# A two-layer decoder on one core: the order of work in the first expert layer and in the fused expert loop

## The chip, the core and the metric

One core of one Trainium2 chip. The metric is the device time in microseconds of one execution; the kernel has one launch. Everything is float32 where it matters here.

## The reference, cut to what matters

A decoder with two post-norm layers over 16 sequences of 64 tokens, 1024 tokens of width 256. Each layer is attention, cross-attention and an expert layer, each followed by a layer norm. The change touches the two expert layers.

```
# layer 0: 8 experts, the best 2 per token, hidden width 1024
probs = softmax(gelu(x @ rw1) @ rw2);  wgt, idx = top_k(probs, 2)
for e in range(8):
    Ye = gelu(x @ w1[e] + b1[e]) @ w2[e] + b2[e]
    Ce = gelu(b1[e]) @ w2[e] + b2[e]              # what a token gets that did not choose e
    for k in range(2):
        mask = idx[..., k] == e;  active = any(mask)
        out += active * wgt[..., k] * where(mask, Ye, Ce)

# layer 1: 64 gates mapped to 8 fused experts of 8 parts each, rank 8, hidden width 176
scores -> top 6 -> w_dense -> flat = w_dense[:, inv_mapping];  scalar = flat.sum(-1);  w = softmax(flat)
fused_linear(x, W, qa, qb, scale, w) = x @ W.T + scale * sum_k w_k * (x @ qa_k) @ qb_k
xe   = x + w @ muW.T
gate = silu(fused_linear(xe, gate...));  up = fused_linear(xe, up...)
y   += scalar * fused_linear(gate * up, down...)
# and a shared expert of width 352 on every token
```

## The kernel before, in words

The program is written engine by engine. TensorE (`pe`), VectorE (`dve`), ScalarE (`act`), GpSimd (`pool`) and SyncE (`sp`, which issues transfers) each run their own list in order, and semaphores (`Signal`) join them. There is no scheduler: the order on an engine is the order in the text. A float32 product is two instructions in the trace, each with a weight load of its own.

**First expert layer.** The router's logits give VectorE the marks of the chosen experts (L2252 to L2263). TensorE counts them (`c["before"]` and `c["ones"]`, L1199 and L1201), VectorE works out a place for each token and two tables, `in_lane` and `in_tile` (L2272 to L2295), and TensorE's product of the two (L1207) is the token list: 23 row tiles (`ROW_TILES`) of 128 tokens sorted by expert. GpSimd gathers each tile's rows (L720) and later scatters the answers (L728). SyncE fetches each tile's first weights (L589).

The constant term is what tokens get of experts they did not choose. `unseen(e)` (L1127) sums gelu(b1) @ w2 for expert e into four column quarters of bank 3; it needs all of `w2`, whose last two experts arrive late (L580). `sum_unseen` (L1136) adds the quarters, VectorE copies the 8 rows to `ceb` (L2331), under which `b2` lies. The weights of tokens (`weight_c`, 16 columns for each token tile) are transposed (L1219) to `wct`, copied by ScalarE (L1833). The counts for "is the expert active at all" are L1211, behind the token list.

Then comes the loop over row tiles (L1224). Tile r: `turn_rows(r+1)` transposes the next tile, `up(r)` makes 32 products into banks 0 and 1, `down(r-1)` 16 into bank 4 or 5. For r from 2 to 9 `turn_rows` also makes the constant term of one token tile (L1151), 16 rows deep, into the second half of its bank, and VectorE adds it to x (L2333).

**Fused expert loop.** 16 steps (`STEPS`), two halves of 512 tokens for each of 8 experts. Step n needs, on TensorE: the x products (`fuse_in`, L1569: w @ muW, 8 rows deep, one product for each half of the width), the rank products a (`ranks`, L1576), the gate and up features g and u and the tails t of both (`features`: L1588 from x, L1592 from the ranks; gate's ranks are rows 0 to 63 and up's 64 to 127), and the outputs (`outputs`: L1613 down's ranks d, over column halves, 128 rows of `h6` and 48 of `ha6`, L1618 and L1622 the sums over both). The list in step s is:

```
fuse_in(step + 1);  features(step);  ranks(step + 1);  outputs(step - 1)
```

All but the output sums go through four banks in turn (`ring`, L525): a product may start when the one four places earlier has been read (`bank_free`, L538). ScalarE reads g and t (silu, L2034), GpSimd scales them (L805), VectorE does the rest in this order: x of step s+1 is added to the tokens (`inputs6`, L2636; at the first half of an expert also L2643 and L2644, which scale its weights), u of s is multiplied with the gate (`hidden6`, L2653), a of s+1 with the weights (`ranks6`, L2661), t of s (L2653 again), d of s-1 (`down_ranks6`, L2669). The transfers of an expert and its mixing weights are issued by SyncE two steps or more ahead (L642, L661, L662). GpSimd clears `ha6` before the loop (L797).

## Time and profile before

| | us |
|---|---|
| median of three runs | 1045.49 |
| the three runs | 1042.62, 1056.3, 1045.49 |
| profiled execution, device time | 1040.52 |
| its span | 1038.6 |

| engine | busy us | share | instructions |
|---|---|---|---|
| TensorE | 958.0 | 92% | 7302 |
| TensorE weight loads | 594.0 | 57% | 7302 |
| VectorE | 541.3 | 52% | 1083 |
| ScalarE | 362.9 | 35% | 729 |
| GpSimd | 213.7 | 21% | 259 |

The span is from the first to the last instruction of the profiled execution; the device time holds some 2 us around it. A line number such as L1588 is the line of the kernel's text. "Busy" of TensorE is from an instruction's start to its modelled end, and neighbours overlap. The chain of waits is followed back from the last instruction: at each step it names what released the engine, or the instruction ahead of it. 68% of this chain is TensorE, 21% VectorE, 4% ScalarE. The mean granted clock of TensorE is 0.974 of its full 2.4 GHz; its lower level is 0.5.

### The profile page before, as it was taken

To read this page: it belongs to the slowest core of one execution; us is meant where nothing else is said; L and a number is where in the kernel's file an instruction comes from. 1 tells how busy PE (TensorE), PEld (TensorE's weight loads), DVE (VectorE), ACT (ScalarE), POOL (GpSimd) and SP (SyncE) were. 2 spreads that over 40 slices of the span, in tenths; PEclk is the share of its full clock that TensorE was granted. 3 is DMA by queue.
4 is the path that set the end of the run, shared out by engine and by line. 5 is a ranking of instruction groups with operands and counts; after the bars stand their busy time and mean duration, and the time that the engine had idled before them with its cause. 6 is when DMAs were issued, how large, how long until landed. Compare 5 with 4: busy or idle time off the path is not lost.

```text
span 1038.6 us, 18579 instructions
## 1 busy us (share of the span) xinstructions
PE 958.0 (92%) x7302; PEld 594.0 (57%) x7302; DVE 541.3 (52%) x1083; ACT 362.9 (35%) x729; POOL 213.7 (21%) x259
## 2 busy tenths in 40 slices
PE   7799899999989999999888899878899999999995
PEld 3665543333458899997554467746554444444453
DVE  2589788988441110113788677758663232332325
ACT  2334536666522223333477245245230000000002
POOL 6011100000012222312125842730000111111110
PEclk9999999999989999999999999999799999999998
DMA  5000330000345555645130201230105033332001
GB/s 210 1 3 1 119 136 2 2 2 2 122 149 211 164 185 177 185 148 171 48 42 1 81 2 42 83 145 3 51 13 128 0 93 93 92 93 88 6 0 42
DMA packets 28602, 81.43 MB, mean 78 GB/s; under 512 B 10068, under 2 KB 17372, under 8 KB 22500
## 3 DMA queue, kind: packets, MB, share of 16 engines
q1 hardware_dynamic: 26308, 74.20, 21.9%
q0 software_dynamic: 2208, 6.03, 1.9%
q8 instruction: 60, 0.98, 0.4%
q14 instruction: 26, 0.21, 0.1%
HBM read 70.62 MB, written 8.55 MB: 76 GB/s over the span
## 4 chain that ended last, share of the span: by engine, by line
PE 68%; DVE 21%; ACT 4%; issue 3%; POOL 2%; DMA 1%; DVEq 0%; SPq 0%; ACTq 0%; POOLq 0%
PE psum L1588 9%; PE psum L1164 8%; PE psum L1176 8%; DVE arena L2185 5%; PE psum L1592 3%; PE psum L878 3%; PE psum L1383 3%; PE psum L1618 3%; PE psum L1576 3%; PE psum L1622 3%; PE psum L1554 2%; PE psum L1062 2%; DVE arena L2102 2%; DVE arena L2101 2%; PE psum L1613 2%
## 5 line engine op out<-in xcount | busy, mean ns | idle before, releaser
L2034 ACT ACTIVATE arena<-psum 128x512 f32<-128x512 f32 (+1 forms) x32 | 19.0, 593 | 219.5 <-PE psum L1592 219.5
L1842 ACT ACTIVATE arena<-psum,arena 128x128 f32<-128x128 f32 x184 | 52.4, 368 | 115.4 <-PE psum L1164 78.5
L1588 PE MATMUL psum<-arena 128*128 128x512 f32 (+1 forms) x192 | 90.6, 608 | 0.5 <-DVE arena L2653 0.5
L805 POOL TENSOR_TENSOR arena<-arena 128x512 f32<-128x512 f32 (+1 forms) x32 | 40.4, 1264 | 234.5 <-ACT arena L2034 234.5
L2185 DVE TENSOR_REDUCE arena<-psum 128x2 f32<-128x512 f32 x128 | 82.5, 688 | 11.0 <-PE psum L1008 9.5
L1164 PE MATMUL psum<-arena 128*128 128x128 f32 x736 | 86.8, 276 | 0.5 <-DVE arena L2328 0.5
L1164 PEld LDWEIGHTS psum<-arena 128*128 128x128 f32 x736 | 84.0, 192 | 3.4 <-issue 2.7
L1176 PE MATMUL psum<-arena 128*128 x368 | 83.4, 378 | 0.0
L2328 DVE COPY arena<-psum 128x256 f32<-128x256 f32 x23 | 9.7, 424 | 136.5 <-PE psum L1149 86.0
L1819 ACT ACTIVATE arena<-psum 128x1024 f32<-128x1024 f32 x64 | 65.3, 1024 | 30.4 <-PE psum L1030 27.1
L1176 PEld LDWEIGHTS psum<-arena 128*128 128x128 f32 x368 | 67.9, 189 | 9.0
L2653 DVE TENSOR_TENSOR arena<-arena,psum 128x512 f32<-128x512 f32 (+1 forms) x32 | 22.1, 689 | 86.9 <-POOL arena L805 86.4
L1588 PEld LDWEIGHTS psum<-arena 128*128 128x128 f32 (+1 forms) x192 | 33.1, 185 | 55.2 <-issue 53.5
L816 PE MATMUL psum<-arena 128*128 128x512 f32 (+1 forms) x118 | 50.9, 554 | 0.0
L1008 PE MATMUL psum<-arena 32*128 32x256 f16 x256 | 44.5, 276 | 5.8 <-DVE arena L2185 2.7
L728 POOL DMA_INDIRECT returned<-arena x23 | 22.7, 987 | 123.5 <-DVE arena L2344 123.5
L2636 DVE TENSOR_TENSOR arena<-psum,arena 128x512 f32<-128x512 f32 x32 | 22.1, 692 | 49.7 <-issue 45.8
L737 POOL TENSOR_TENSOR arena<-arena 128x512 f32<-128x512 f32 x32 | 32.9, 1054 | 45.9 <-ACT arena L1900 27.4
L878 PE MATMUL psum<-arena 64*128 64x256 f32 x256 | 33.1, 399 | 6.5 <-DVE arena L2132 5.9
L1062 PE MATMUL psum<-arena 128*32 128x256 f32 x512 | 35.1, 393 | 0.6 <-ACT arena L1819 0.5
L1592 PE MATMUL psum<-arena 64*128 64x512 f32 (+1 forms) x96 | 34.4, 625 | 0.0
L816 PEld LDWEIGHTS psum<-arena 128*128 128x128 f32 (+1 forms) x118 | 19.3, 169 | 26.2 <-issue 25.8
(357 smaller groups left out, 1764.2 us busy)
## 6 DMA issues: line engine op xcount, KB each, us to landing
arena<-in_w SPq DMA_DIRECT2D x31, 1024.0 KB, 9.9
arena<-in_experts SPq DMA_DIRECT2D x8, 1248.0 KB, 6.0
arena<-mixed SPq DMA_DIRECT2D x16, 256.0 KB
arena<-mixed SPq DMA_DIRECT2D x8, 512.0 KB, 9.3
arena<-returned SPq DMA_DIRECT2D x8, 256.0 KB, 4.5
kept<-arena SPq DMA_DIRECT2D x2, 1024.0 KB, 7.8
arena<-kept SPq DMA_DIRECT2D x2, 1024.0 KB, 5.9
arena<-in_w_ffn SPq DMA_DIRECT2D x1, 1152.0 KB, 5.1
```

Of the source, the lines that this page charges most:

```text
L805: do(pool.tensor_tensor(out=g6[rows, 2 * half + i, :], in0=g6[rows, 2 * half + i, :], in1=scale6[rows, f % BUFS, cols], op=ALU.mult), scaled6)
L816: pe.matmul(bank(spare), eye, wide(eye, 1, BANK // P), start=True, stop=True)
L878: last = pe.matmul(replicated(u, p)[:, g * D:(g + 1) * D], w[rows, g, :], qr[rows, u % 2, i, :], start=(i == 0), stop=(i == 1), tile_posit ...
L1008: last = pe.matmul(bank(u % 2)[:, tc * D:(tc + 1) * D], stack["q"][r0:r1, b, g, tc * P:(tc + 1) * P], stack["k"][r0:r1, b, g, :], start=Tr ...
L1062: last = pe.matmul(bank(6)[32 * q:32 * q + 32, 0:D], vx[:, b, sc, q, 32 * g:32 * g + 32], ptx[:, (n + q // 2) % 4, q % 2, sc, :], start=(g ...
L1164: last = pe.matmul(bank(n)[:, i * P:(i + 1) * P], w1_tile[:, r % 2, k, features], xst[:, r % 2, k, :], start=(k == 0), stop=(k == KC - 1))
L1176: last = pe.matmul(bank(4 + r % 2)[:, 0:D], hidt[:, r % 2, ic * P:(ic + 1) * P], w2v[:, bass.ds(e, 1), ic, :], start=(ic == 0), stop=(ic = ...
L1588: pe.matmul(out, e[w][:, k, :], xe6[:, half, k, :], start=(k == 0), stop=False)
L1592: mid_ps.by(pe.matmul(out, qb6[r0:r1, n // 2 % 2, q0:q0 + m], aw6[r0:r1, half, :], start=False, stop=True))
L1819: ptx_ready.by(act.activation(ptx[:, n % 4, :, :, :].rearrange("p a b c -> p (a b c)"), bank(2 + 2 * (n % 2), 2), ACT.Exp, scale=float(DHX ...
L1842: last = act.activation(hidt[:, r % 2, ic * P:(ic + 1) * P], bank(n)[:, i * P:(i + 1) * P], ACT.Gelu, bias=b1_tile[:, r % 4, ic:ic + 1])
L2185: ax_max.by(dve.tensor_reduce(nmx[:, b % 2, :, h], bank(u % 2).rearrange("p (t s) -> p t s", t=2), AX.X, ALU.max, negate=True))
```

## The change

In the first expert layer: the counts L1211 and `unseen(6)` go ahead of the token list's product, `unseen(7)` and two products without a use follow it (`keep_clock`). The transposed weights, `ceb` and `b2` now exist four times, one in each row quarter, so that the constant terms of four token tiles are four products side by side (`const_rows`); there are two such groups, in tiles 2 and 4, and VectorE adds each in two instructions (`add_const`). In the fused loop: `fuse_in(step + 1)` moves into `features`, between the rank products of g and u and the tails. Its two operands move from rows 0 and 32 to row halves, with zeros up to 64 rows, for which GpSimd clears `wm6`, and the 48 rows of `dqat` and `ha6` become 128. The ring's order follows.

```diff
--- before.py
+++ after.py
@@ -66,7 +66,7 @@
 
 EXPERT = [("gw", P, (KC, P)), ("uw", P, (KC, P)), ("tw", P, (KC, TAILS)), ("qa", P, (KC, P)),
           ("qb", P, (P + TAILS,)), ("qs", P, (P + TAILS,)), ("dw", P, (D,)), ("dwx", P, (D,)),
-          ("dqa", P, (KX * RX,)), ("dqat", TAIL, (KX * RX,)), ("ds", P, (D,)), ("mu", 32 + KX, (P,))]
+          ("dqa", P, (KX * RX,)), ("dqat", P, (KX * RX,)), ("ds", P, (D,)), ("mu", P, (P,))]
 
 
 def columns(parts):
@@ -311,6 +311,7 @@
         ce4_sb = again("ce4_sb", ov0_sb, B)
         ce_sum = again("ce_sum", o0_ps, B)
         tiles_ready = again("tiles_ready", q_sb, 6)
+        const_ps = again("const_ps", elu_ready, 1)
         rows_out = signal("rows_out")
         xs_in = [signal("xs_in_even"), signal("xs_in_odd")]
         xst_ps = again("xst_ps", mem_ps, NT)
@@ -386,8 +387,8 @@
         ti1_blank = again("ti1_blank", lg_ps, 1)
         unit_act = again("unit_act", p_exp, 1)
         unit_pool = again("unit_pool", p_sub, 1)
-        rest_ps = again("rest_ps", wct_ps, 2)
-        rm1_ready = again("rm1_ready", wct_sb, 2)
+        rest_ps = again("rest_ps", wct_ps, 1)
+        rm1_ready = again("rm1_ready", wct_sb, 4)
         solve_ps = again("solve_ps", cnt_ps, 2)
         xv_act = again("xv_act", ce_ps, 1)
         xv_dve = again("xv_dve", ceb_sb, 1)
@@ -522,7 +523,7 @@
         STEPS = 2 * FX
         ring, by_dve, by_act = {}, {}, {}
         for step in range(-1, STEPS + 1):
-            for kind, n in (("x", step + 1), ("g", step), ("u", step), ("t", step), ("a", step + 1), ("d", step - 1)):
+            for kind, n in (("g", step), ("u", step), ("x", step + 1), ("t", step), ("a", step + 1), ("d", step - 1)):
                 for k in range(KC if kind == "x" else 1):
                     if 0 <= n < STEPS:
                         ring[(kind, k), n] = len(ring)
@@ -576,7 +577,8 @@
                 fetch_expert(e, w12_early)
             sp.wait_ge(x_norm.sem, 2 * NT)
             sp.dma_start(a["rows"].rearrange("(j p) d -> p j d", p=P), x).then_inc(rows_out.sem, 16)
-            sp.dma_start(ceb[E0:2 * E0, :], a["b2"]).then_inc(b2_in.sem, 16)
+            for q in range(4):
+                sp.dma_start(ceb[32 * q + E0:32 * q + 2 * E0, :], a["b2"]).then_inc(b2_in.sem, 16)
             for e in range(len(EARLY), E0):
                 fetch_expert(e, w12_in[e])
             b1_at = columns(PACKS["w_route0"][:2])
@@ -640,7 +642,7 @@
                 mixed, buf = a["mixed"], f % BUFS
                 few = mixed[f * KX:(f + 1) * KX, :]
                 for k in range(KC):
-                    sp.dma_start(wm6[32 * k:32 * k + KX, buf, :], few).then_inc(near_in[buf].sem, 16)
+                    sp.dma_start(wm6[64 * k:64 * k + KX, buf, :], few).then_inc(near_in[buf].sem, 16)
                 for half in range(2):
                     sp.dma_start(we6[64 * half:64 * half + 64, buf, :], wide(few, 1, RX)).then_inc(mix_in[buf].sem, 16)
                 sp.dma_start(scale6[:, buf, :], mixed[FX * KX + f:FX * KX + f + 1, :].to_broadcast([P, B * S]))\
@@ -654,6 +656,7 @@
                     sp.wait_ge(wt6_sb.sem, wt6_sb.base + 2)
                     sp.dma_start(a["mixed"], wt6[0:FX * KX + FX, :]).then_inc(mixed_out.sem, 16)
                     sp.wait_ge(mixed_out.sem, 16)
+                    sp.wait_ge(tail_blank.sem, 1)
                     for near in range(BUFS):
                         fetch_mix(near)
                     continue
@@ -794,6 +797,7 @@
                 pool.wait_ge(xt_ps.sem, 2 * NT + j + 1)
                 x_beta.by(pool.tensor_tensor(out=x[:, j, :], in0=x[:, j, :], in1=x1["beta"], op=ALU.add))
             pool.wait_ge(x_norm.sem, 5 * NT)
+            do(pool.memset(wm6.rearrange("p a n -> p (a n)"), 0.0))
             do(pool.memset(ha6.rearrange("p a n -> p (a n)"), 0.0), tail_blank)
             for n in range(STEPS):
                 f, half = n // 2, n % 2
@@ -1135,22 +1139,29 @@
 
             def sum_unseen():
                 pe.wait_ge(ce4_sb.sem, ce4_sb.base + 1)
-                ce_sum.by(pe.matmul(bank(2)[0:E0, 0:D], c["selmax"][:, 0:E0, 0], ce4, start=True, stop=True))
+                for q in range(4):
+                    last = pe.matmul(bank(2)[32 * q:32 * q + E0, 0:D], c["selmax"][:, 0:E0, 0], ce4, start=True, stop=True,
+                                     tile_position=(0, 32 * q))
+                ce_sum.by(last)
 
             def turn_rows(r):
                 pe.wait_ge(xs_in[r % 2].sem, xs_in[r % 2].base + 16 * (r // 2 + 1))
                 if r >= 2:
                     pe.wait_ge(xst_sb.sem, xst_sb.base + r - 1)
-                if r == 2:
-                    pe.wait_ge(ceb_sb.sem, 1)
-                if 4 <= r < NT + 4:
-                    pe.wait_ge(const_read.sem, r - 3)
+                if r in (4, 6):
+                    pe.wait_ge(const_read.sem, r - 2)
                 for k in range(KC):
                     last = pe.transpose(bank(6 + r % 2)[:, k * P:(k + 1) * P], xs[:, r % 2, k * P:(k + 1) * P], ident)
-                if 2 <= r <= NT + 1:
-                    last = pe.matmul(bank(6 + r % 2)[:, D:2 * D], wct[0:2 * E0, (r - 2) * P:(r - 1) * P], ceb[0:2 * E0, :],
-                                     start=True, stop=True)
                 xst_ps.by(last)
+
+            def const_rows(half):
+                pe.wait_ge(ceb_sb.sem, 1)
+                pe.wait_ge(xst_sb.sem, xst_sb.base + 2 * half + 4)
+                for q in range(4):
+                    rows, b, at = slice(32 * q, 32 * q + 2 * E0), (2, 3, 6, 7)[q], (0, 0, D, D)[q]
+                    last = pe.matmul(bank(b)[:, at:at + D], wct[rows, half * P:(half + 1) * P], ceb[rows, :], start=True,
+                                     stop=True, tile_position=(32 * q, 0))
+                const_ps.by(last)
 
             def up(r):
                 pe.wait_ge(w1_in[r % 2].sem, w1_in[r % 2].base + 32 * (r // 2 + 1))
@@ -1201,35 +1212,40 @@
             cnt_ps.by(pe.matmul(bank(6)[:, 0:E0 * (NT + 1)], c["ones"], earlier[:, :, 0:NT + 1], start=False, stop=True))
             for e in EARLY[3:]:
                 unseen(e)
+            for j in range(NT):
+                last = pe.matmul(bank(5)[:, 0:2 * E0], c["ones"], marks[:, j, :], start=(j == 0), stop=(j == NT - 1))
+            cnt_ps.by(last)
+            pe.wait_ge(w12_in[6].sem, w12_in[6].base + 16)
+            unseen(6)
             for half in range(2):
                 pe.wait_ge(lanes_ready.sem, half + 1)
                 for n in range(half * NT, (half + 1) * NT):
                     last = pe.matmul(bank(4)[:, 0:ROW_TILES], in_lane[:, n, :], in_tile[:, n, :], start=(n == 0),
                                      stop=(n == 2 * NT - 1))
             spots_ps.by(last)
-            for j in range(NT):
-                last = pe.matmul(bank(5)[:, 0:2 * E0], c["ones"], marks[:, j, :], start=(j == 0), stop=(j == NT - 1))
-            cnt_ps.by(last)
-            for e in range(len(EARLY), E0):
-                pe.wait_ge(w12_in[e].sem, w12_in[e].base + 16)
-                unseen(e)
+            pe.wait_ge(w12_in[7].sem, w12_in[7].base + 16)
+            unseen(7)
+            keep_clock(2, 7)
             pe.wait_ge(wc_ready.sem, 1)
             for i in range(2):
-                for t in range(4):
-                    last = pe.transpose(bank(i)[0:2 * E0, t * P:(t + 1) * P], weight_c[:, 4 * i + t, :], ident)
-                wct_ps.by(last)
+                for q in range(4):
+                    last = pe.matmul(bank(0)[32 * q:32 * q + 2 * E0, i * P:(i + 1) * P], weight_c[:, 4 * i + q, :], ident,
+                                     start=True, stop=True, tile_position=(0, 32 * q))
+            wct_ps.by(last)
             pe.wait_ge(tiles_ready.sem, tiles_ready.base + 1)
-            pe.wait_ge(b2_in.sem, b2_in.base + 16)
+            pe.wait_ge(b2_in.sem, b2_in.base + 64)
             turn_rows(0)
             for r in range(ROW_TILES + 1):
                 if r + 1 < ROW_TILES:
                     turn_rows(r + 1)
                 if r == 0:
-                    pe.wait_ge(wct_sb.sem, 2)
+                    pe.wait_ge(wct_sb.sem, 4)
                 if r < ROW_TILES:
                     up(r)
                 if r == 0:
                     sum_unseen()
+                if r in (2, 4):
+                    const_rows(r // 2 - 1)
                 if r >= 1:
                     down(r - 1)
             def project5(u):
@@ -1565,7 +1581,7 @@
                 for k in range(KC):
                     bank_free(pe, (("x", k), n))
                 for k in range(KC):
-                    rows = slice(32 * k, 32 * k + KX)
+                    rows = slice(64 * k, 64 * k + 64)
                     mid_ps.by(pe.matmul(bank(ring[("x", k), n] % 4), ex[f % BUFS]["mu"][rows, :], wm6[rows, f % BUFS, cols],
                                         start=True, stop=True))
 
@@ -1597,6 +1613,8 @@
                 pe.wait_ge(qb6_ready.sem, qb6_ready.base + 2 * (n // 2) + 2)
                 from_ranks(gate, 0, 64, 0, P)
                 from_ranks(up, 64, P, 0, P)
+                if n + 1 < STEPS:
+                    fuse_in(n + 1)
                 from_ranks(from_x("t", "tw", TAILS), 0, P, P, TAILS)
 
             def tile_sum(j):
@@ -1611,7 +1629,7 @@
                     for u in range(2):
                         cols = slice(u * D, (u + 1) * D)
                         last = pe.matmul(bank(ring[key] % 4)[64 * u:64 * u + 64, 0:D], e[("dqa", "dqat")[i]],
-                                         (h6[:, half, cols], ha6[0:TAIL, half, cols])[i],
+                                         (h6, ha6)[i][:, half, cols],
                                          start=(i == 0), stop=(i == 1))
                 mid_ps.by(last)
                 for t in range(4):
@@ -1673,9 +1691,7 @@
             shared_down(1, (2, 3))
             pe.wait_ge(tail_blank.sem, 1)
             for step in range(STEPS + 1):
-                if step + 1 < STEPS:
-                    fuse_in(step + 1)
-                if 0 <= step < STEPS:
+                if step < STEPS:
                     features(step)
                 if step + 1 < STEPS:
                     ranks(step + 1)
@@ -1828,10 +1844,10 @@
                 r1_sb.by(act.activation(r1[:, n * BANK:(n + 1) * BANK], bank(2 + n), ACT.Gelu))
             act.wait_ge(p_sub.sem, 1)
             p_exp.by(act.activation(prob, prob, ACT.Exp))
-            for i in range(2):
-                act.wait_ge(wct_ps.sem, i + 1)
-                wct_sb.by(act.activation(wct[0:2 * E0, i * BANK:(i + 1) * BANK], bank(i)[0:2 * E0, :],
-                                         ACT.Copy))
+            act.wait_ge(wct_ps.sem, 1)
+            for q in range(4):
+                rows = slice(32 * q, 32 * q + 2 * E0)
+                wct_sb.by(act.activation(wct[rows, 0:2 * P], bank(0)[rows, 0:2 * P], ACT.Copy))
             for r in range(ROW_TILES):
                 if r >= 2:
                     act.wait_ge(down_ps.sem, down_ps.base + r - 1)
@@ -2328,15 +2344,24 @@
                 xst_sb.by(dve.tensor_copy(xst[:, r % 2, :, :].rearrange("p k t -> p (k t)"), bank(6 + r % 2)[:, 0:D]))
                 if r == 1:
                     dve.wait_ge(ce_sum.sem, ce_sum.base + 1)
-                    do(dve.tensor_copy(ceb[0:E0, :], bank(2)[0:E0, 0:D]), ceb_sb)
-                if 2 <= r <= NT + 1:
-                    const_read.by(dve.tensor_tensor(out=x[:, r - 2, :], in0=bank(6 + r % 2)[:, D:2 * D],
-                                                    in1=x[:, r - 2, :], op=ALU.add))
+                    for q in range(4):
+                        last = dve.tensor_copy(ceb[32 * q:32 * q + E0, :], bank(2)[32 * q:32 * q + E0, 0:D])
+                    do(last, ceb_sb)
+
+            def add_const(half):
+                dve.wait_ge(const_ps.sem, const_ps.base + half + 1)
+                for i, at in enumerate((0, D)):
+                    tiles = slice(4 * half + 2 * i, 4 * half + 2 * i + 2)
+                    const_read.by(dve.tensor_tensor(
+                        out=x[:, tiles, :], in0=bank((2, 6)[i], 2).rearrange("p (t c) -> p t c", t=2)[:, :, at:at + D],
+                        in1=x[:, tiles, :], op=ALU.add))
 
             copy_rows(0)
             for r in range(ROW_TILES + 2):
                 if r + 1 < ROW_TILES:
                     copy_rows(r + 1)
+                if r in (2, 4):
+                    add_const(r // 2 - 1)
                 if r >= 2:
                     dve.wait_ge(down_ps.sem, down_ps.base + r - 1)
                     if r >= 4:
@@ -2839,8 +2864,10 @@
             "qa": chunks(np.concatenate([rank("L1_ffn_gate_qa", f), rank("L1_ffn_up_qa", f)], 1)),
             "qb": fused(unrank("L1_ffn_gate_qb", f), unrank("L1_ffn_up_qb", f)), "qs": fused(*scales),
             "dw": dw[:P], "dwx": np.concatenate([dw[P:], np.zeros((64 - TAIL, D), np.float32), unrank("L1_ffn_down_qb", f)]),
-            "dqa": dqa[:P], "dqat": dqa[P:], "ds": every(g["L1_ffn_down_scale"][f]),
-            "mu": np.concatenate([mu[:, :P], np.zeros((32 - KX, P), np.float32), mu[:, P:]])}))
+            "dqa": dqa[:P], "dqat": np.concatenate([dqa[P:], np.zeros((P - TAIL, KX * RX), np.float32)]),
+            "ds": every(g["L1_ffn_down_scale"][f]),
+            "mu": np.concatenate([part for half in (mu[:, :P], mu[:, P:])
+                                  for part in (half, np.zeros((64 - KX, P), np.float32))])}))
     w["experts"] = np.stack(experts)
     w["x"] = g["x"].reshape(B * S, D)
     w["x_t"] = chunks(w["x"].T)
```

## Rows read from the trace of the kernel before

**Rows 1.** Chain of waits, one pass of the fused loop: start us, us, engine, line, count.

```profile
860.30 1.06 PE psum L1569 x4
861.36 3.63 PE psum L1588 x8
864.99 1.06 PE psum L1592 x4
866.05 1.90 PE psum L1588 x4
867.95 0.86 PE psum L1592 x2
868.81 1.72 PE psum L1576 x4
870.53 1.16 PE psum L1613 x8
871.69 1.92 PE psum L1618 x8
```

**Rows 2.** Timeline, the same pass, other engines: start us, us, engine, line, operation, idle before.

```profile
861.45 1.42 DVE L2636 TENSOR_TENSOR arena<-psum,arena 128x512 f32<-128x512 f32 x2 [3.54 <-issue]
...
863.34 0.42 DVE L2644 TENSOR_TENSOR arena<-arena 64x256 f32<-64x256 f32 x1
...
866.08 0.60 ACT L2034 ACTIVATE arena<-psum 128x512 f32<-128x512 f32 x1 [11.68 <-PE psum L1592]
...
866.82 1.26 POOL L805 TENSOR_TENSOR arena<-arena 128x512 f32<-128x512 f32 x1 [11.01 <-ACT arena L2034]
...
868.22 0.19 PEld L1576 LDWEIGHTS psum<-arena 128*128 128x128 f32 x1 [0.25 <-issue]
```

**Rows 3.** Timeline, TensorE, the loop's first turn.

```profile
801.15 3.27 PE L1588 MATMUL psum<-arena 128*128 128x512 f32 x7 [0.52 <-DVE arena L2653]
```

**Rows 4.** Chain of waits at the same place.

```profile
801.15 3.70 PE psum L1588 x8
```

**Rows 5.** Chain of waits, first expert layer.

```profile
307.01 0.42 DVE arena L2331
...
324.14 0.62 PE psum L1151 x2
324.76 3.77 PE psum L1164 x32
...
379.88 3.57 PE psum L1164 x32
```

**Rows 6.** Windows: length, busy PE, PEld, DVE, ACT, POOL (count), clock, DMA share, GB/s.

```profile
288.60:291.10 2.50, 0.02 (x1) 0.03 (x2) 2.36 (x6) 0.00 (x0) 0.00 (x0) 1.00 0.20 33
292.60:296.30 3.70, 3.70 (x24) 3.70 (x24) 1.65 (x8) 0.00 (x0) 1.60 (x2) 0.50 0.96 338
```

**Rows 7.** Chain of waits, from the token list to the first row tile.

```profile
292.99 3.42 PE psum L1211 x16
296.41 3.53 PE psum L1130 x32
...
302.63 3.81 PE psum L1164 x32
```

**Rows 8.** Timeline, TensorE, row halves in the first layer's attention.

```profile
119.57 2.00 PE L878 MATMUL psum<-arena 64*128 64x256 f32 x16
```

**Rows 9.** Timeline, TensorE, row quarters.

```profile
537.79 1.17 PE L1311 MATMUL psum<-arena 32*128 32x128 f32 x32
```

**Rows 10.** Timeline, GpSimd, the second gather.

```profile
295.86 0.95 POOL L720 DMA_INDIRECT arena<-rows,arena  x1 [0.30 <-issue]
```

**Rows 11.** All gathers of L720: issue to landing.

```profile
DMA to landing us min/median/max: 2.7/2.8/3.8
```

**Rows 12.** Timeline, GpSimd and VectorE, side by side.

```profile
583.14 3.04 POOL L737 TENSOR_TENSOR arena<-arena 128x512 f32<-128x512 f32 x3
...
584.39 0.69 DVE L2430 TENSOR_TENSOR arena<-psum,arena 128x512 f32<-128x512 f32 x1
```


## The prediction

> **What bounds the kernel now.** I read the chain of waits first. In the fused expert loop it never leaves TensorE: one pass of the loop is nine groups of products with no other engine between them [rows 1]. A full product of 512 columns takes two instructions of 0.43 us (four in 1.72, L1576), one of 256 columns two of 0.215. Against that the groups split by rows or columns of the array are dear where they meet the others: the x products (L1569) do four instructions two at a time, 2 x 0.43 = 0.86, and take 1.06; the eight full ones behind them should take 3.43 and take 3.63; the rank products L1592 (1.06) and the four behind them (1.90 for 1.72) show the same. So each island of row-split products costs about 0.40 beyond its streaming, 0.20 going in and 0.20 coming out. The reader should see that a step holds three islands: x, the gate and up ranks, and the column-split L1613.
>
> Then the timeline of the other engines in the same step [rows 2]: VectorE adds the x products 0.09 after their end, ScalarE takes the gate 0.03 after the ranks' end at 866.05, GpSimd's scaling ends at 868.08. All is idle enough today. The first turn of the loop is the exception: TensorE waits 0.52 there for VectorE [rows 3].
>
> In the first expert layer the chain is TensorE's too [rows 5]: a row tile with its constant term pays 0.62 for L1151 and 3.77 where a later tile pays 3.57 for the same 32 products, 0.82 in all, eight times. Before its first tile the windows show 2.5 us in which TensorE is all but idle, and behind it a granted clock of 0.50, the 1.2 GHz level [rows 6], in which L1211 and L1130 take 3.42 and 3.53 [rows 7].
>
> **The loop, part by part.** *x products between the ranks and the tails.* Both now use row halves 0 to 63 and 64 to 127, so two islands become one: 0.40 saved in each of the 15 steps that have an x product, 6.0 us. This takes for granted that four row-split passes follow one another without exposing their weight loads. The nearest row is sixteen 64-row instructions of 256 columns in 2.00 us [rows 8]: 8 x 0.215 = 1.72, and the rest is the way in and the last one's end. Nothing is exposed between them. The Trainium skill (TensorE: Matmul & The Clock Gate, "The mechanism" in Part 3) says that a weight load overlaps running products only when its row group differs. By it each further pass pair on the same halves would expose a load; the trace disagrees, since there loads and products alternate on the same two halves.
>
> *Zero rows instead of 48- and 8-row operands.* Rows cost no time, columns do. L1613 takes 1.16 and what follows it 1.92 [rows 1], where streaming is 4 x 0.215 + 8 x 0.215 = 2.58: 0.50 of excess, 0.10 more than the 0.40 of an island. I put that 0.10 down to the turn from 128 to 48 rows inside it, gone now: 16 x 0.1 = 1.6 us (between 0 and 2.4). The expert's transfer keeps its size, since the packed array already held 128 rows. The clearing of wm6 on GpSimd lies before the loop, in a stretch where that engine idles, and costs nothing; if it did not, SyncE's new wait on it would hold up the first mixes.
>
> *The ring of four banks.* Its order becomes g, u, x, x, t, a, d. The first turn no longer stops: g(1) now needs only x(1) read, not the tail t(0). Today that wait comes behind an x group, and goes: 0.5. Two new waits appear. t(n) needs g(n) read by ScalarE: 0.63 after the ranks' end, while the x products keep TensorE for 0.86. Covered. And a(n+1) needs u(n) read by VectorE (L2653). I lay one step out on the clock of [rows 1, 2]. Ranks end 866.05, x products 866.91, tails (1.90 + 0.86) 869.67; a's first weights would load 0.59 ahead of its slot as now (868.22 [rows 2] for 868.81 [rows 1]), at 869.08. VectorE adds x from 867.00 to 868.42 and only then, by its own order, multiplies u: 868.45 to 869.14 (0.69, as a sum of this shape has in [rows 12]). That is 0.06 late for the load and still 0.3 before the slot at 869.67: no loss. But when the next step starts an expert, L2643 and L2644 stand between (862.87 to 863.76, 0.89): u is read at 870.03. Behind such a wait eight products took 3.70 instead of 3.43 [rows 4], 0.27 from the release. So a streams from 870.03 + 0.04 + 0.27 = 870.34, 0.67 late. Seven steps are so (n+1 = 2, 4, ... 14): 4.7 us lost. Bounds: 0 if TensorE's queue or a short step covers it, 7 x 0.9 = 6.3 if the whole 0.89 shows. Behind a, VectorE and TensorE are late together, and nothing more is lost.
>
> Loop: 6.0 + 1.6 + 0.5 - 4.7 = 3.4 us gained.
>
> **The first expert layer.** *Constant term in two groups.* Removed: 8 x 0.82 = 6.6. Added: twice four products of 256 columns on four row quarters at once. A row for four quarters in float32 is 32 instructions of 128 columns in 1.17 [rows 9]: 8 x 0.107 = 0.86 and the way in. So a group is 0.43 + 0.40 = 0.83, two of them 1.7. Saved 4.9; if the four did not overlap, 2 x (1.71 + 0.4) = 4.2 would leave 2.4. VectorE's four additions of 128x512 (0.69 each) replace eight; they put off the copy of ys(0) and ys(2) by a product group, some 6 us, and with it a scatter and a gather on GpSimd's queue, but the gather is wanted two tiles later, over 10 us off. down(2) needs ys(0) a whole tile later too.
>
> *The wait for ceb.* turn_rows(2) waited for L2331 (0.42, with a hand-over of some 0.06 on either side [rows 5]); now not: 0.55 saved, less 0.1 for the four-quarter sum. VectorE's three further copies (3 x 0.42) end within up(1).
>
> *Counts ahead of the token list.* L1211 fills the idle 2.5 us [rows 6]; at the full level it is half of 3.42, 1.7, and the 16 instructions of expert 6 are a quarter of what 3.53 bought, 0.9. So they end near 291.3, before the second half of the lanes, whose product ends where L1211 starts today, at 292.99 [rows 7], and the list is not late. In front of expert 6's weights stand three more small transfers on SyncE's queue; today they are long there when used. Behind the list there is expert 7 (0.9) and two clock products (1.7), then the eight small products, now on column quarters. By then the gathers decide: the second is issued at 295.86 [rows 10] and lands after 2.8 to 3.8 [rows 11], so it is there at 298.7 to 299.7. up(0), today at 302.63 [rows 7], starts near 299.6: 3.0 saved. From it I take 0.8 for the clock, which may still be granted low for a stretch, as the engine stays thinly used until 299: 2.2 (0.5 to 3.5).
>
> Layer: 4.9 + 0.45 + 2.2 = 7.5 us.
>
> **Sum.** 3.4 + 7.5 = 10.9 us. The profiled execution took 1040.5 (span 1038.6), so 1029.6; the median of the runs, 5 us above it, goes to 1045.5 - 10.9 = 1034.6.
>
> **The rivals.**
> A, the late u costs nothing (chance 0.16): for it speaks that 0.67 hangs on the order of three short operations. Then 4.7 more is gained: 1030.
> B, the clock stays at 1.2 GHz until 301 anyway, and the first tile runs partly at it (0.20): for it, L1211's products are thin and would not make the engine look busy; against it, the idle stretch is filled. The head gains 0.5 instead of 2.2 and the first tile's 3.8 lose 1 to 2: 1037 to 1038.
> C, row-split passes on the same halves expose their loads (0.06): 0.19 twice per step, 15 x 0.38 = 5.7 gone: 1040. The sixteen instructions of [rows 8] speak against it. This is also where the loop change would do nothing it says.
> D, slower (0.04): VectorE's x additions now fall on GpSimd's scaling (866.82 to 868.08), which today runs alone. If the two excluded each other, the additions would start at 868.08, u be read at 870.22 in even and 871.11 in odd steps, and a stream 0.9 and 1.8 late: 8 x 0.9 + 7 x 1.8 = 19.8 instead of 4.7. The loop loses 11.7, the layer gains 7.5: 1050. It turns to a loss from 1.0 us per step on. Against it: an addition from PSUM took 0.69 in the midst of GpSimd's products, as alone, and those 3 x 1.01 [rows 12]. [...]
>
> **Chances.** Forecast 0.54 (1034.6, on its own 1029 to 1040 by the bounds and the 3 us between the two lower runs shown), A 0.16, B 0.20, C 0.06, D 0.04. The range 1025 to 1042 takes in A, B and C with a spread of some 3 to 5 us and leaves D and outliers. 2% of the time is 21 us, about what a measurement of this kernel can tell from no change: faster by over 2% needs 1024.6, below A with all bounds (0.05); slower by over 2% is beyond D (0.01); within 2% 0.94.
>
> **What would show it.** Right: L1569 directly behind L1592, eight row-split instructions in about 1.9 us; L1588's gate products without a gap behind L1622; a wait of L1576 for L2653 of about 0.6 in seven steps, none in the eight others; L1613 nearer 1.06; two groups of constant products and 3.57 for every tile's up products; up(0) near 299.6; full clock between 291 and 299. Wrong: GpSimd's scaling longer than 1.26, VectorE's additions longer than 0.69, a wait of the lanes' product for expert 6's weights, or a gather that up(5) waits for.

## The result, and the profile after

The changed kernel takes 1037.3 us in the median of four runs (1031.6 to 1040.23); the kernel before, beside it on the same chip, took 1048.31 (1042.62 to 1056.3). The ratio is 0.9897, with a 95% interval from 0.9855 to 0.9938: about 10.8 us less, forecast 10.9. A second comparison, on another chip, gave 0.9898 [0.9851, 0.9945]. The profiled execution took 1031.6 (span 1029.8) against 1040.52 (span 1038.6), 8.9 less.

To see where they lie I cut each trace at four places: the start of the token list's product ("list"), the first up product of the first row tile, the start of the last down product of the last one, and the loop from its first product on the experts' input to the start of its last product on the tokens ("from x", L1604). Times between them, in us:

| kernel | list to first up | row tiles | row tiles to loop | loop | rest |
|---|---|---|---|---|---|
| before | 11.5 | 174.3 | 304.2 | 235.4 | 22.2 |
| after | 8.2 | 168.8 | 307.1 | 232.2 | 22.2 |
| difference | -3.3 | -5.5 | +2.9 | -3.2 | 0.0 |

The differences come to -9.1, and the list starts 0.3 later than before: -8.8, the difference of the spans. (Some expectations below count the loop only to the start of the last step's gate products, some 5.9 us less: 229.5 before, 226.3 after.)

**The loop.** The chain of waits of the changed kernel, one whole step and the next up to its wait (start us, us, engine, line, count). It answers to [rows 1].

```profile
808.77 3.43 PE psum L1604 x8
812.20 1.06 PE psum L1608 x4
813.26 0.86 PE psum L1585 x4
814.12 1.90 PE psum L1604 x4
816.02 0.86 PE psum L1608 x2
816.88 1.72 PE psum L1592 x4
818.60 1.01 PE psum L1631 x8
...
828.70 0.70 DVE arena L2661
...
829.43 0.70 DVE arena L2661
...
830.15 0.42 DVE arena L2668
...
830.59 0.43 DVE arena L2669
...
831.05 0.70 DVE arena L2678
...
831.88 1.95 PE psum L1592 x4
```

The reader should see two things. L1585, the x products, stands directly behind the rank products L1608 and costs its bare 0.86; the way in (1.06) and out (1.90) is paid once for both, and the full products after a step's start are 3.43 where they were 3.63. And in every other step the chain leaves TensorE: VectorE adds x twice (L2661), scales the new expert's weights (L2668, L2669), only then multiplies u (L2678), and the a products (L1592) start when that is done. How long GpSimd's scaling took (ns: least, median, most):

```profile
L809 POOL TENSOR_TENSOR arena<-arena x32: 1259/1264/1282, 789.0 to 1009.9; 128x512 f32<-128x512 f32 x16, 48x512 f32<-48x512 f32 x16
```

In seven of the loop's 16 groups of L1592 TensorE stood idle for VectorE, as forecast. GpSimd's 1.264 us is what [rows 2] had before (1.26), with VectorE's additions on top of it now and a maximum of 1.282. In the step shown the scaling runs for 1.28 us from 828.53 and the two additions for 1.42 from 828.70: the two engines do not exclude each other here.

**The first expert layer.** Its chain, answering to [rows 5]: two tiles' products and the first group of constant terms (the second, at 330.53, is the same).

```profile
307.91 3.47 PE psum L1187 x16
...
311.60 3.57 PE psum L1175 x32
315.17 0.64 PE psum L1162 x8
315.81 3.67 PE psum L1187 x16
```

The up products take 3.57 in every tile but the first. A group of four constant terms (L1162) is 0.64, and the down products behind it pay 0.20 more than 3.47: 0.84 a group, twice, in place of eight times 0.82.

The head, answering to [rows 7], and two windows (length, busy PE, PEld, DVE, ACT, POOL, clock, DMA share, GB/s), answering to [rows 6]:

```profile
292.98 1.83 PE psum L1134 x16
294.81 2.50 PE psum L820 x4
...
297.93 0.37 ACT arena L1850
...
299.13 0.39 ACT arena L1850
...
299.56 3.84 PE psum L1175 x32
```

```profile
292.50:295.90 3.40, 3.31 (x26) 1.38 (x27) 2.50 (x14) 0.00 (x0) 1.22 (x2) 0.51 1.00 370
295.90:299.30 3.40, 2.81 (x24) 1.09 (x22) 0.93 (x3) 1.29 (x4) 1.20 (x2) 0.99 0.47 170
```

The counts and expert 6 are done by 291.4, as laid out. The granted clock was low for 3.4 us (10.2 us before, 291.3 to 301.6), and the first up product starts at 299.56, forecast 299.6. But the gather, by which the forecast had set this time, does not end the head in this profile: it let the first turn of rows (L1154) start at 298.33. The chain runs through expert 7 (L1134), the two clock products (L820), the eight small products and ScalarE's four copies of the transposed weights (L1850), one behind the other until 299.52.

**What is given back.** Between the row tiles and the loop TensorE's code is unchanged, and this stretch is 2.9 us longer. (GpSimd's new clearing of `wm6` lies in it, but "loop alone" below has it too and shows the old 304.2.) Where: TensorE's timeline of the changed kernel, then of the one before, at the same place of the second layer (start us, us, engine, line, operation, tiles, idle before).

```profile
486.33 0.96 PE L830 MATMUL psum<-arena 128*128 128x128 f32 x4 [3.34 <-ACT arena L1719]
...
489.05 3.62 PE L1292 MATMUL psum<-arena 128*128 128x512 f32 x4
492.46 1.81 PE L1295 MATMUL psum<-arena 128*128 128x272 f32 x4
```

```profile
494.88 0.93 PE L826 MATMUL psum<-arena 128*128 128x128 f32 x4 [3.35 <-ACT arena L1703]
...
497.59 2.86 PE L1276 MATMUL psum<-arena 128*128 128x512 f32 x4
500.29 1.08 PE L1279 MATMUL psum<-arena 128*128 128x272 f32 x4
```

The same eight product instructions, behind the same idle 3.3 us, take 3.62 and 1.81 where they took 2.86 and 1.08. The granted clock is at its lower level for 6.8 us there (487.1 to 493.9), for 3.4 us before. At 674.48 eight products of L1259 take 5.37 where the same eight took 3.67, in another such stretch:

```profile
487.10:490.50 3.40, 2.53 (x8) 1.59 (x7) 3.00 (x9) 2.08 (x7) 0.00 (x0) 0.50 0.32 135
...
674.80:678.20 3.40, 3.40 (x5) 1.35 (x4) 2.63 (x9) 0.33 (x2) 1.01 (x2) 0.50 0.15 22
```

The first place costs 1.4 us and the second 1.7; shifts elsewhere give some 0.3 back. The lower level does not last longer in all: from the last down product to the loop it is 27.3 us in both traces. What differs is what runs in it. In the kernel before one such stretch stood at 653.1, and a wait behind it took up what it cost; now one stands at 674.8, on eight full products.

### The profile page after: what moved, and what is told of

It reads as the page before. It is cut to its first block, busy times and chain, and to the rows that moved or that the text cites. A ratio compares the mean times of both kernels' runs of the same rounds, so it can differ in the third digit from the quotient of the medians.

```text
span 1029.8 us, 18623 instructions
## 1 busy us (share of the span) xinstructions
PE 947.2 (92%) x7320; PEld 593.0 (58%) x7320; DVE 543.0 (53%) x1082; ACT 363.8 (35%) x731; POOL 215.9 (21%) x260
## 4 chain that ended last, share of the span: by engine, by line
PE 61%; DVE 25%; issue 8%; ACT 4%; POOL 1%; DMA 1%; DVEq 0%; SPq 0%; ACTq 0%; POOLq 0%
PE psum L1175 8%; PE psum L1187 8%; DVE arena L2201 5%; PE psum L1604 5%; PE psum L1399 3%; PE psum L882 3%; PE psum L1592 3%; PE psum L1636 2%; PE psum L1570 2%; PE psum L1066 2%; DVE arena L2118 2%; DVE arena L2117 2%; PE psum L1608 2%; PE psum L1259 2%; PE psum L1640 1%
## 5 line engine op out<-in xcount | busy, mean ns | idle before, releaser
L1604 PE MATMUL psum<-arena 128*128 128x512 f32 (+1 forms) x192 | 89.1, 600 | 0.0
L2661 DVE TENSOR_TENSOR arena<-psum,arena 128x512 f32<-128x512 f32 x32 | 22.1, 692 | 111.6 <-issue 99.6
L1604 PEld LDWEIGHTS psum<-arena 128*128 128x128 f32 (+1 forms) x192 | 34.3, 185 | 44.4 <-issue 32.3
L820 PE MATMUL psum<-arena 128*128 128x512 f32 (+1 forms) x122 | 53.3, 560 | 0.0
L820 PEld LDWEIGHTS psum<-arena 128*128 128x128 f32 (+1 forms) x122 | 20.2, 173 | 27.6 <-issue 27.2
L1608 PE MATMUL psum<-arena 64*128 64x512 f32 (+1 forms) x96 | 34.4, 625 | 0.0
L1592 PE MATMUL psum<-arena 128*128 128x512 f32 x64 | 30.6, 600 | 3.6 <-DVE arena L2678 3.6
```

What stands on the lines that cost most here:

```text
L820: pe.matmul(bank(spare), eye, wide(eye, 1, BANK // P), start=True, stop=True)
L1592: last = pe.matmul(bank(ring[("a", 0), n] % 4), ex[n // 2 % BUFS]["qa"][:, k, :], xe6[:, n % 2, k, :], start=(k == 0), stop=(k == KC - 1))
L1604: pe.matmul(out, e[w][:, k, :], xe6[:, half, k, :], start=(k == 0), stop=False)
L1608: mid_ps.by(pe.matmul(out, qb6[r0:r1, n // 2 % 2, q0:q0 + m], aw6[r0:r1, half, :], start=False, stop=True))
```

## The experiments

Ten kernels ran, one of them the changed kernel again. Where no median is named, the time is that of one run. Most are read at the four places, since one run's whole time moves by several us with the clock:

| kernel | us | list to first up | row tiles | row tiles to loop | loop |
|---|---|---|---|---|---|
| loop alone | 1041.24 | 11.5 | 174.3 | 304.2 | 232.0 |
| layer alone | 1046.79 | 9.0 | 168.8 | 308.4 | 235.4 |
| changed kernel again | 1034.99 (median of 6) | 8.9 | 168.8 | 308.5 | 232.2 |
| scales later | 1031.13 (median of 6) | 8.7 | 171.3 | 308.5 | 226.9 |
| x at rows 0 and 32 | 1043.06 | 8.7 | 168.8 | 308.6 | 235.2 |
| u ahead of x | 1053.97 | 7.7 | 168.8 | 308.0 | 243.2 |
| counts behind | 1036.72 | 10.8 | 168.8 | 308.0 | 232.2 |
| 48 rows | 1040.6 | 8.7 | 168.8 | 308.4 | 234.1 |
| without filler | 1047.21 | 8.6 | 171.3 | 308.5 | 232.2 |
| filled | 1023.57 (median of 6) | 9.0 | 168.8 | 303.2 | 226.9 |

**The two halves of the change apart.** One kernel has the loop's edits alone, one the first layer's alone.

```diff
 # loop alone: ring order, row halves, 128 rows, and
+                if n + 1 < STEPS:
+                    fuse_in(n + 1)
 # layer alone: counts first, const_rows, add_const, keep_clock
```

> The fused loop as changed, the first expert layer as before. My theory (islands of row-split products cost 0.40 each, the late u 0.7 in seven steps) gives the loop 226.3 us from the first x products to the last step's gate products, 3.2 less than the 229.5 of before, and up(0) at 302.6 with 8.1 us per row tile while constant terms last. Rival: part of the loop's gain comes from its place in time or from the clock; then it is off by over 0.5 us from 226.3.

> The first expert layer as changed, the fused loop as before. My theory: the layer's last down product ends 8.5 us earlier than before (near 468.8), up(0) at 299.6, and the loop takes 229.5 as before. Rival (the two parts help each other, or the layer's gain is given back in the stretch behind it by a lower granted clock): the loop's start then is less than 8 us earlier than before's 781.2, with the same number of row tiles' time, and the difference stands in the granted clock between 480 and 780.

The loop's length goes with the loop's edits (232.0 and 235.4), the row tiles' with the layer's (174.3 and 168.8); they are independent. The whole times, 1041.24 and 1046.79, would tell the opposite of the truth about the layer: it came out slower than the kernel before's profiled run, though it saves 8 us where it acts. Its clock was at the lower level for 20.5 us from 50.0 on and for 13.7 us from 155.8, in code that no edit touches. And the third column: with the loop alone it is 304.2, with the layer alone 308.4. The give-back in the second layer comes with the first layer's edits. ("Counts behind" below, with the head in its old order, still has 308.0, so it is not the head's order that brings it.)

**The late u.** VectorE scales the new expert's weights after u instead of before it.

```diff
+            def scales6(n):
                 f, half = n // 2, n % 2
                 if half == 0:
                     e = ex[f % BUFS]
...
                 if step + 1 < STEPS:
+                    scales6(step + 1)
                     ranks6(step + 1)
```

> The changed kernel with one thing moved: VectorE scales an expert's weights (0.89 us in two operations) after it has multiplied u, not before. If the wait in seven steps is the scaling standing before u, all seven waits of 0.75 go: the loop takes 226.3 - 5.3 = 221.0 us and every step 14.5. If the wait came from ScalarE's or GpSimd's part of u, or from the bank order, the loop stays at 226.3. If half goes, the u multiplication itself is late too. Against the kernel before some 1.5% faster.

The ratio is 0.9826 [0.977, 0.9882]. The loop is 226.9, 5.3 less than 232.2; expected 5.3. All steps are alike in its chain now, but for one that takes 14.67:

```profile
815.90 1.72 PE psum L1592 x4
817.62 1.01 PE psum L1631 x8
818.63 1.92 PE psum L1636 x8
...
833.12 1.92 PE psum L1636 x8
```

From one L1636 to the next it is 14.49 us, with no wait. So the stall was the two short scalings ahead of u and nothing else.

**The row split.** The x products go back to rows 0 and 32, in their new place behind the ranks.

```diff
-                    rows = slice(64 * k, 64 * k + 64)
+                    rows = slice(32 * k, 32 * k + KX)
```

> The changed kernel with the x products' operands where they were before, 8 rows at rows 0 and 32, but in their new place behind the rank products. If the 0.40 of an island is paid for each change between ways of splitting the array, a change from 64-row to 32-row splitting costs too, and the step loses 0.1 to 0.2: the loop takes 227.8 to 229.3. If only the change between whole and split costs, the loop stays at 226.3 and the zero rows bought nothing.

The loop is 3.0 longer. I had taken an island to be an island; the chain shows that inside one a turn from 64-row to 32-row pieces has a price too:

```profile
851.18 1.06 PE psum L1608 x4
852.24 1.06 PE psum L1585 x4
```

L1585 is 1.06 in place of 0.86: 0.20 in each of 15 steps is 3.0. So of the 6.0 us that the joined island brings, half needs the rows 0 and 64 and the zeros (not tried apart), and the order alone would have brought the other half.

**The order u before x.** VectorE multiplies u first. The line shown is the count of VectorE's operations, by which the others wait for it; the order of the banks stays.

```diff
-            for kind, n in (("x", step + 1), ("u", step), ("a", step + 1), ("t", step), ("d", step - 1)):
+            for kind, n in (("u", step), ("x", step + 1), ("a", step + 1), ("t", step), ("d", step - 1)):
```

> The changed kernel with VectorE multiplying u before it adds the x products, in every step. If the rank products a wait for VectorE's order (my theory), now the x sums are late: they end near 4.4 us behind the rank products, a streams 1.06 late in all 15 steps, the scaling is behind both, and the loop takes 221.0 + 15.9 = 237 us. Rival, that a is held by the bank alone: then u is read early, no step waits, and the loop takes 221.

The loop is 11.0 longer, forecast 10.7: the other way round is worse, because u waits for GpSimd's scaling, and the additions of x then wait behind u.

```profile
857.90 1.28 POOL arena L809
...
859.37 0.70 DVE arena L2678
...
860.81 0.70 DVE arena L2661
...
861.56 1.98 PE psum L1592 x4
```

**48 rows again.** The second half of the down products on the ranks reads 48 rows, as before the change.

```diff
-    e[("dqa", "dqat")[i]], (h6, ha6)[i][:, half, cols],
+    (e["dqa"], e["dqat"][0:TAIL, :])[i], (h6[:, half, cols], ha6[0:TAIL, half, cols])[i],
```

> The changed kernel with one part of it undone: the second half of the down products on the ranks reads 48 rows again instead of 128 (the padded rows are loaded, and not read). In the profile of the changed kernel the eight products of a step took 1.01 us, before 1.16 us. Theory one: changing the number of rows between products of one group is what cost the 0.15 us, so the group takes 1.16 us again and the loop is 0.15 x 16 = 2.4 us longer, at 234.5 us from its first product on the experts' input to the last from-x product, against 232.1. Theory two: the 0.15 us came from something else (the new order of the products around the group), the group stays at 1.01 us and the loop at 232.1. The time of the whole kernel says little: one run moves by several us with the granted clock.

The group is back at its old time, to the hundredth:

```profile
825.82 1.16 PE psum L1631 x8
```

The loop is 234.1, 1.9 longer, not 2.4: of the 16 groups 14 lie inside the stretch that I measure, and 14 x 0.15 = 2.1. A group of 128 and 48 rows costs more than one of 128 and 128.

**Counts behind the list again.** The layer's head in its old order and without the two clock products, the constant groups kept.

> The changed kernel with the head's order as before: counts and both late experts behind the token list, no clock products; constant terms stay in groups. Theory: TensorE idles 2.5 us before the lanes, the clock falls to 0.5 near there, counts and the two experts take 3.4 and 3.5 us, and from the token list's product to the first row tile's up products there are 10 us instead of 6.8 to 8.5 (11.5 before). Rival: the gathers decide anyway, and it stays at 8 or less.

From the list to the first up product it is 10.8, against 8.2 and 8.9 in the two profiles of the changed kernel; the head's low stretch lasts 6.8 us there, and the counts and expert products pay for it at half clock in its chain:

```profile
294.85 3.42 PE psum L1222 x16
298.27 3.31 PE psum L1134 x32
```

**Without the filler.** `keep_clock(2, 7)` is left out.

```diff
             unseen(7)
-            keep_clock(2, 7)
             pe.wait_ge(wc_ready.sem, 1)
```

> The changed kernel without its keep_clock(2, 7), the filler products between the last unused-expert products and the transposes of the combine weights. Theory one (clock): TensorE waits there for the weights, the granted clock falls or stays low behind it, and the eight transposes, the first up product's row turns and the products after them run at half clock; the first up product then starts 1 to 3 us later after the counts than the 8.2 us of the changed kernel, and a low stretch of the granted clock reaches past 296 us. Theory two (the filler does nothing): from the start of the counts to the first up product it stays 8.2 us, or is up to 0.5 us shorter because the filler no longer stands in the queue.

Neither theory holds as written. The head (from the list to the first up product) takes 8.6 us, within the 7.7 to 9.0 of the eight profiles with the filler. The lower level does last longer, 10.2 us, and runs into the first tile:

```profile
306.30:309.70 3.40, 1.05 (x16) 0.49 (x16) 1.24 (x5) 1.26 (x4) 1.41 (x2) 0.50 0.76 290
309.70:313.10 3.40, 2.96 (x13) 2.62 (x14) 0.78 (x2) 1.52 (x2) 1.89 (x2) 0.50 0.14 39
```

and the tiles take 171.3 where eight profiles have 168.8. But "scales later", which has the filler, shows 171.3 too, with a low stretch of 6.8 us at the head; in the seven other profiles with the filler it lasts 3.4 us at most. One run can't say whether the filler prevents this or chance did. Nor does its head gain anything by the missing filler, since the gather ends it. In its chain the gather stands as one piece of 4.17 us ahead of the first turn of rows:

```profile
305.58 4.17 DMA arena<-rows,arena
```

The seven other profiles with the filler have a gather in their chain at this place too. Only the first profile of the changed kernel has the filler there instead, and in it the turns of rows were done at 299.26, 0.3 before the first up product: an estimate from these two times of the most that the filler can have cost.

**Filled.** "Scales later", with fillers on TensorE ahead of four idle places: two products before each of the last two `replicate` calls of the attention, three before `turn_x(2)`, one before and one within `turn_x(3)`.

```diff
                 if u >= NT - 1:
+                    keep_clock(2, 7)
...
+            keep_clock(3, 7)
             turn_x(2, range(4))
...
+                    keep_clock(1, 7)
                     turn_x(3, range(0, 1))
             turn_x(3, range(1, 2))
+            keep_clock(1, 7)
             turn_x(3, range(2, 4))
```

> The version with the scaling moved, and eight further products without a use (512 columns, 0.85 us each) put into four places where TensorE otherwise waits: two before each of the last two copies of queries in the first layer's attention (near 42 and 46 us), three before the second layer's first transposes (near 483), one each before the first and the third transposed tile ahead of the query projection (near 669). Theory: these are the places behind which the granted clock falls to 0.5, for 3.4 to 20.5 us, and the low stretches there carry the spread between executions and what the layer's change gave back. Then the stretch from 17 to 300 us is some 5 us shorter than in the executions with the 20.5 us low stretch, the stretch from the last down product to the loop's start is 304 us or less instead of 307 to 308, and the time is 5 to 9 us below the version without the fillers. Rival: the low stretches come from elsewhere; then nothing moves, or the fillers add up to 1 us each where they are in the way.

> The changed kernel unaltered, timed beside the others. Both theories: about 10 us (1%) below the kernel before; its last down product to its loop's start 307 us or more if what the layer gave back belongs to its place against the clock, 304 if that was chance.

Filled has 1023.57 us and the ratio 0.977 [0.9729, 0.9811], the fastest of all: 11.4 us below the changed kernel on the same chip. 5.3 of it is the loop, as in "scales later"; 5.3 is the stretch between row tiles and loop, 303.2 against 308.5. Laid beside "scales later", whose code is the same but for the fillers, 2.5 of these 5.3 are won at the first place of fillers and 1.5 near 675, behind the other two. The last 1.3 lie near 746, where no new filler stands and the clock rises earlier in the code; that the fillers cause this too is not shown. At the first place the products that took 3.62 and 1.81 run at the full level:

```profile
485.43 2.84 PE L820 MATMUL psum<-arena 128*128 128x512 f32 x6
...
491.19 1.94 PE L1295 MATMUL psum<-arena 128*128 128x512 f32 x4
492.97 1.08 PE L1298 MATMUL psum<-arena 128*128 128x272 f32 x4
```

```profile
492.20:495.60 3.40, 3.40 (x11) 1.81 (x10) 2.39 (x9) 1.37 (x4) 0.70 (x1) 1.00 0.00 0
```

Its six runs lie between 1021.0 and 1025.0, those of the changed kernel beside it between 1032.0 and 1041.3. The fillers at 41.8 and 45.6 us may be why the spread is smaller. Its profile has no low stretch from 48 to 73 us, where six others have one of 20.5 or 23.9; but the changed kernel has only 6.8 us, from 60 on, in its own two profiles without these fillers. The interval of the ratio overlaps that of "scales later", so it is the stretch, and not the whole time, that shows what the fillers bring.

## Why the prediction was right

The forecast, 1034.6 us and 10.9 less, stands against 1037.3 and 10.8 less. The 2.7 between the two times comes with the kernel before: its median moved from 1045.49 to 1048.31 when a fourth run, 1051.13, joined the three. That 10.8 and 10.9 lie so close is luck. The interval of the ratio allows 6.5 to 15.2 us, the profiles differ by 8.9, and one loss of 2.9 us had no term in the forecast. What was right is the mechanism of the loop and of the row tiles. Step by step:

- **Joined islands**, forecast 15 x 0.40 = 6.0, and **128 rows in L1613**, forecast 0.10 a step. A step without a stall is 14.49 us; a pass of the kernel before averages 15.03 (30.07 for two). That is 0.55: 0.40 and 0.15. The first term was exact, the second 0.05 a step too small, and over the 14 groups inside the stretch it is 2.1 and not 1.6; "48 rows" confirms the 0.15 by itself.
- **The first turn's wait**, forecast 0.5: gone.
- **The late u**, forecast 7 x 0.67 = 4.7. Two steps together take 29.73, so the stall is 29.73 - 2 x 14.49 = 0.75, and 5.3 in all; "scales later" gave 5.3 back. Mechanism and place were right, so rival A was wrong. The forecast put u's end 0.04 and a load before the stream; here u ends at 831.75 and a streams about 0.13 + 0.23 later, 0.36 in all against 0.31, and the rest is small shifts of VectorE's series.
- **Loop together.** 6.0 + 14 x 0.15 + 0.5 - 5.3 = 3.3. Measured is 3.3 with the loop alone (235.35 less 232.01) and 3.2 in the changed kernel, forecast 3.4. The two errors of size, +0.5 and -0.6, cancel.
- **Constant term**, forecast 4.9 by 0.83 a group: 0.84 measured. With the 0.45 for `ceb`, 5.35 was forecast for the tiles and 5.5 measured.
- **Head**, forecast 3.0 less 0.8 for the clock. The first up product came 3.1 earlier in this pair, and the low stretch was over at 295.9, so the 0.8 taken off for the clock was too much. The term was 0.9 too small in this pair, and the 299.6 was met by another path than the one laid out: ScalarE's copies ended the head, not the gather, as the chain above shows. In the seven other profiles with the filler the gather did end it, with pieces of 2.9 to 4.8 us in the chain; over the eight profiles with the new order and the filler the head is 7.7 to 9.0, so 2.5 to 3.8 better than 11.5, and "counts behind" gets all but 0.7 of it back. Rival B had a low clock until 301 and the first tile half at it. It did not happen in the profile of the changed kernel, but it does happen: "scales later" shows the tiles at 171.3 with the low level from 308.3 to 315.2.
- **What no step had.** The layer saved 8.5 (forecast 7.5), and 2.9 came back in the second layer, where I had let everything stand. Sum of the profiles: 8.9, forecast 10.9. The nine profiles with the new constant groups and without the extra fillers have 307.1 to 308.6 there; the two kernels with the old ones both have 304.2. That it is the granted clock is shown, by products of unchanged shape at half rate and by the fillers that remove it. Why the first layer's edits bring it is open. TensorE's code ahead of the place is the same, and the idle time too (3.34 and 3.35). The time at which the place comes does not explain it: with the layer alone the eight products start at 499.71, between the 497.59 of the kernel before and the 501.63 of "loop alone", and are slow in it alone.
- **Rivals C and D.** Loads of four row-split passes on the same halves are not exposed: L1608 and L1585 follow one another in 1.06 + 0.86, which is eight times 0.215 and one way in, and L1585's first weights load at 812.67, while L1608's products fill both halves until 813.26. The Trainium skill (TensorE: Matmul & The Clock Gate, "The mechanism" in Part 3), by which a load overlaps only with products on another row group, is not borne out here. GpSimd's scaling was unchanged at 1.264.

## What to carry to other kernels

Put products that split the array alike next to one another, and give them equal pieces, with zeros if need be: here each change of the split cost 0.20 us, a change of the number of rows in a group 0.15 in all, and zero rows nothing that shows. When a product moves forward, lay out the order of the engine that reads it, operation by operation; two scalings of 0.42 us ahead of the one that frees a bank cost 5.3 of the 6.5 us that the move saved. Judge a part of a change at checkpoints in the trace, not by the whole time, and look for what it gives back in code that it does not touch.

## What the runs showed of the hardware that I had not expected

- Inside a run of row-split products, the turn from 64-row to 32-row pieces cost 0.20 us, as much as the turn from the whole array. The Trainium skill (TensorEngine Tiling (Array Packing), "Key Properties") says that a change of the tiling mode drains the engine. The runs agree in that no weights were loaded ahead across such a change, and put a price to it. The x products' first loads, with rows 0 and 32 and then in the changed kernel:

```profile
852.17 0.30 PEld L1585 LDWEIGHTS psum<-arena 8*128 8x128 f32 x4 [0.76 <-issue]
```

```profile
812.67 0.19 PEld L1585 LDWEIGHTS psum<-arena 64*128 64x128 f32 x2 [0.24 <-issue]
```

  The rank products ahead of them end at 852.24 and 813.26: behind a change of split the loads start 0.07 us before that end, without one 0.59 before it.
- The granted clock behind the same code is not the same in each run. Behind an idle 2.38 us near 46 us, the same 32 products took 2.43 us in the kernel before and 3.73 in "loop alone" (its lower level lasted 20.5 us there, in the other 3.4), while TensorE was busy all the time (20.50 of the 20.50 us of "loop alone"):

```profile
48.25 3.10 PE L878 MATMUL psum<-arena 64*128 64x256 f32 x16 [2.38 <-DVE arena L2132]
...
51.59 2.43 PE L893 MATMUL psum<-arena 64*128 64x64 f32 x32
```

```profile
48.60 2.81 PE L880 MATMUL psum<-arena 64*128 64x256 f32 x16 [2.38 <-DVE arena L2134]
...
51.65 3.73 PE L895 MATMUL psum<-arena 64*128 64x64 f32 x32
```

- Where the fillers stand in an idle place in the middle of the kernel they cost nothing that shows and bring 4.0 us where they stand, 5.3 in the whole stretch; in the head one run could not tell their effect from none.
